# A Trainium2 kernel of four fused blocks: the engines' loops written out as straight code

## The reference

```python
# 1. attention, 16 heads of 8, LayerNorm on each head's q and k, causal
dot = jnp.einsum('bqhs,bkhs->bhqk', q, k) * scale
attn = jax.nn.softmax(jnp.where(causal, dot, -jnp.inf), axis=-1)
out = jnp.einsum('bhqk,bkhs->bqhs', attn, v).reshape(b, t, e) @ Wo + bo
# 2. soft mixture of experts, 8 experts x 64 slots
logits = jnp.einsum('bnd,esd->bnes', xn, sn)
dispatch = jax.nn.softmax(logits, axis=1)
combine = jax.nn.softmax(logits.reshape(b, n, e * s), axis=-1)
slots = jnp.einsum('bnd,bnes->besd', xn, dispatch)
h = gelu(jnp.einsum('besd,edh->besh', slots, w1) + b1)
out = jnp.einsum('bmd,bnm->bnd', (h @ w2 + b2), combine)
# 3. differential attention: softmax(q1 k1) - lam * softmax(q2 k2), times v, RMS norm
# 4. attention over the batch axis, then a routed mixture (top 2 of 8 experts, capacity 1280):
probs = softmax(x @ router_weight); top_p, top_i = top_k(probs, 2)
exp_out = gelu(exp_in @ moe_w1) @ moe_w2          # per expert
```

## Time and profile before

| | us |
|---|---|
| median of 3 runs (range) | 1091.5 (1090.92 to 1092.26) |
| profiled execution: span from first to last instruction | 1086.1 |
| PE busy | 919.8 |
| DVE busy | 712.3 |
| ACT busy | 625.7 |
| POOL busy | 569.8 |

### The profile page before, as it was taken

The page is one execution under the profiler, slowest core; times in us unless marked ns, Lnnn a source line. Parts: engine busy times, 40 slices in busy tenths (PEclk is TensorE's granted clock), DMA queues, the critical chain, the costliest instruction groups (busy, mean ns, idle before and its releaser), DMA issues.

```text
span 1086.1 us, 20632 instructions
## 1 busy us (share of the span) xinstructions
PE 919.8 (85%) x6577; PEld 615.8 (57%) x6614; DVE 712.3 (66%) x1512; ACT 625.7 (58%) x1129; POOL 569.8 (52%) x645
## 2 busy tenths in 40 slices
PE   7688879988999899899999868677788886999980
PEld 4366654477555555555555446454555655998870
DVE  6788852125777677677766565999857673646374
ACT  6466664421887687678778746344478664333320
POOL 3400019261675566656642217999306771888772
PEclk9899989999999999999999969879989998999995
DMA  5011111434010010100101049900011102223277
GB/s 144 1 78 78 77 79 58 135 128 135 21 31 21 22 30 21 31 21 21 30 21 30 2 79 149 298 11 0 1 39 43 51 28 79 83 78 92 73 204 219
DMA packets 83841, 74.46 MB, mean 69 GB/s; under 512 B 6786, under 2 KB 76876, under 8 KB 81712
## 3 DMA queue, kind: packets, MB, share of 16 engines
q1 hardware_dynamic: 73392, 64.03, 22.3%
q0 software_dynamic: 4608, 6.64, 1.9%
q10 hardware_dynamic: 5760, 2.70, 0.9%
HBM read 34.14 MB, written 33.70 MB: 62 GB/s over the span
## 4 chain that ended last, share of the span: by engine, by line
PE 32%; DVE 18%; POOL 10%; issue 9%; ACT 2%; DMA 1%; ACTq 0%; DVEq 0%; POOLq 0%
PE banks L2030 6%; PE banks L2002 5%; PE banks L2016 5%; POOL y_dram L975 4%; PE banks L2056 3%; DVE B_mneg L1150 2%; PE banks L2004 2%; DVE D_dmx L1282 2%; PE banks L2114 2%; PE banks L2069 2%; PE banks L2165 1%; DVE banks L1331 1%; DVE D_sc L1308 1%; POOL x L951 1%; DVE D_pr L1293 1%
## 5 line engine op out<-in xcount | busy, mean ns | idle before, releaser
L1150 DVE TENSOR_REDUCE B_mneg<-banks 128x2 f32<-128x256 f32 (+3 forms) x256 | 208.5, 824 | 76.9 <-PE banks L2004 68.3
L1669 ACT ACTIVATE B_pt<-banks 128x1024 f32<-128x1024 f32 (+3 forms) x256 | 178.7, 708 | 72.9 <-PE banks L2016 67.8
L792 POOL TENSOR_SCALAR_AFFINE_SELECT B_pt<-B_pt 128x512 f32<-128x512 f32 x128 | 81.2, 634 | 170.4 <-ACT B_pt L1669 161.3
L2002 PE MATMUL banks<-B_kp,B_qt 128*128 128x128 bf16 (+3 forms) x507 | 124.7, 299 | 1.8 <-DVE B_mneg L1150 0.6
L2016 PE MATMUL banks<-B_qt,B_kp 128*128 128x256 bf16 (+3 forms) x480 | 105.2, 297 | 12.1 <-issue 5.2
L2004 PE MATMUL banks<-B_mask_q,B_identb 128*128 128x128 bf16 x512 | 101.8, 219 | 0.7 <-issue 0.6
L2030 PE MATMUL banks<-B_pt,B_vp 128*32 128x512 f32 (+3 forms) x1024 | 95.5, 445 | 1.4 <-ACT B_ot L1675 0.7
L1819 ACT ACTIVATE F_gh<-banks 128x512 f32<-128x512 f32 (+1 forms) x96 | 50.0, 526 | 78.8 <-PE banks L2234 74.2
L930 POOL DMA_INDIRECT rows_dram<-F_xs,F_rowi x64 | 62.4, 975 | 60.2 <-issue 59.6
L2165 PE MATMUL banks<-D_qk 128*128 128x512 f32 x128 | 74.9, 671 | 10.2 <-DVE D_pr L1293 10.2
L975 POOL DMA_INDIRECT y_dram<-F_yo,F_ide x60 | 60.8, 1014 | 37.8 <-DVE F_yo L1510 17.4
(11 more groups left out here) (292 smaller groups left out, 2192.3 us busy)
## 6 DMA issues: line engine op xcount, KB each, us to landing
comb_dram<-C_comb SPq DMA_DIRECT2D x8, 1024.0 KB, 3.9
C_cst<-comb_dram SPq DMA_DIRECT2D x8, 1024.0 KB, 4.8
B_kp<-B_kt SPq DMA_DIRECT2D x64, 128.0 KB, 2.4
rows_dram<-D_zeros SPq DMA_DIRECT2D x8, 650.0 KB, 17.8
F_xe<-rows_dram SPq DMA_DIRECT2D x8, 650.0 KB, 3.9
C_w<-w_in SPq DMA_DIRECT2D x16, 256.0 KB, 2.9
y_dram<-D_zeros SPq DMA_DIRECT2D x2, 2048.0 KB, 19.0
F_gw<-mw_in SPq DMA_DIRECT2D x16, 256.0 KB, 3.0
```

The lines of the kernel that those rows point to most:

```text
L792: g.affine_select(out=w, in_=w, compare_op=ALU.is_ge, fill=0.0, base=0, pattern=[[0, G], [1, P]], channel_multiplier=-1).then_inc(B_md, 1)
L1150: v.tensor_reduce(mneg[:, g % 2, qt, 2 * hp:2 * hp + 2], banks2[pair_of_banks(item)][:, :, 0:(qt + 1) * P], X, ALU.max, negate=True).then_ ...
L1669: a.activation(pt[:, 2 * hp:2 * hp + 2, PT_AT[kt]:PT_AT[kt] + w], banks2[pair_of_banks(item)][:, :, 0:w], ACT.Exp).then_inc(B_ex, 1)
L2002: t_.matmul(dst, qt1[:, g % 2, hp, qt * P:(qt + 1) * P], kp[:, g % NG, hp, h, 0:(qt + 1) * P], start=True, stop=False)
```

## The change

All seventeen `Fori` loops, on SP, POOL, DVE, ACT and PE, become Python `for` loops, so that the bodies are written out once per iteration. The same items run in the same order with the same buffers, semaphores and counts; thresholds and addresses are constants. `Chain` loses its loop bookkeeping. `Rounds.place` now tells the last round by its number, where before any integer counted as that. The core of the diff (the other loops are edited the same way):

```diff
@@ class Chain
     def __init__(self, eng, sem):
-        self.eng, self.sem, self.start, self.n, self.it, self.per = eng, sem, 0, 0, 0, 0
-
-    def loop(self, it, per):
-
-        self.start, self.n, self.it, self.per = self.start + self.n, 0, it, per
-
-    def end_loop(self, times):
-        assert self.n == self.per, (self.n, self.per)
-        self.start, self.n, self.it, self.per = self.start + times * self.per, 0, 0, 0
+        self.eng, self.sem, self.n = eng, sem, 0
 
     def link(self, ins):
 
         self.n += 1
         ins.then_inc(self.sem, 1)
-        self.eng.wait_ge(self.sem, self.it * self.per + (self.start + self.n))
+        self.eng.wait_ge(self.sem, self.n)
...
+LAST_ROUND = B // 2 - 1
...
     def place(self, stream, it, item):
 
         names = self.streams[stream]
-        if isinstance(it, int) and it >= 0:
+        if it == LAST_ROUND:
             names = [x for x in names if x not in self.early]
         return names.index(item) + 1
...
             dve_round_c(-1, True)
-            with dve.Fori(0, B // 2 - 1) as it:
-                own.loop(it, 2 * (1 + 1 + 2))
+            for it in range(B // 2 - 1):
                 dve_round_c(it, False)
-            own.end_loop(B // 2 - 1)
             dve_round_c(B // 2 - 1, False, True)
...
-            with act.Fori(0, EXP // 2) as pr:
+            for pr in range(EXP // 2):
                 for par in range(2):
...
             pe_round(-1, True)
-            with pe.Fori(0, B // 2 - 1) as it:
+            for it in range(B // 2 - 1):
                 pe_round(it, False)
             pe_round(B // 2 - 1, False, True)
...
             pe_round_g(-1, True)
-            with pe.Fori(0, EXP // 2 - 1) as it:
+            for it in range(EXP // 2 - 1):
                 pe_round_g(it, False)
             pe_round_g(EXP // 2 - 1, False, True)
```

More of the change, by code:

```diff
@@ L625, in store_comb @@
                                  comb[:, par, :, :].rearrange("p m n -> p (m n)")).then_inc(C_cw[par], 16)
-            with sp.Fori(0, B // 2 - 1) as hb:
+            for hb in range(B // 2 - 1):
                 store_comb(hb)
             store_comb(B // 2 - 1)
-            with sp.Fori(1, EXP // 2) as pr:
+            for pr in range(1, EXP // 2):
                 for par in range(2):
@@ L661, in _ @@
             spread_keys(-1, True)
-            with sp.Fori(0, B // 2 - 1) as it:
+            for it in range(B // 2 - 1):
                 spread_keys(it, False)
@@ L859, in _ @@
             pool_round(-1, True)
-            with pool.Fori(0, B // 2 - 1) as it:
-                own.loop(it, 2 * 2 * 6)
+            for it in range(B // 2 - 1):
                 pool_round(it, False)
-            own.end_loop(B // 2 - 1)
             pool_round(B // 2 - 1, False, True)
@@ L1125, in _ @@
             dve.sem_inc(C_pp, 2)
-            with dve.Fori(0, EXP // 2) as pr:
+            for pr in range(EXP // 2):
                 for par in range(2):
@@ L1231, in _ @@
             dve_round(-1, True)
-            with dve.Fori(0, B // 2 - 1) as it:
-                own.loop(it, PG * 3 + 2 * 4)
+            for it in range(B // 2 - 1):
                 dve_round(it, False)
-            own.end_loop(B // 2 - 1)
             dve_round(B // 2 - 1, False, True)
@@ L1519, in _ @@
             dve_round_g(-1, True)
-            with dve.Fori(0, EXP // 2 - 1) as it:
-                own.loop(it, 2 * (2 * 3 + 2))
+            for it in range(EXP // 2 - 1):
                 dve_round_g(it, False)
-            own.end_loop(EXP // 2 - 1)
             dve_round_g(EXP // 2 - 1, False, True)
@@ L1623, in _ @@
             act_round_c(-1, True)
-            with act.Fori(0, B // 2 - 1) as it:
+            for it in range(B // 2 - 1):
                 act_round_c(it, False)
@@ L1820, in _ @@
             act_round_g(-1, True)
-            with act.Fori(0, EXP // 2) as it:
+            for it in range(EXP // 2):
                 act_round_g(it, False)
@@ L1933, in _ @@
             pe.sem_inc(C_ps, 2)
-            with pe.Fori(0, EXP // 2) as pr:
+            for pr in range(EXP // 2):
                 for par in range(2):
```

## The result

| | before | after |
|---|---|---|
| median, first comparison (4 runs each) | 1091.21 us (1088.66 to 1092.26) | 1074.25 us (1072.77 to 1076.21) |
| ratio after/before | | 0.985, interval 0.9833 to 0.9867 |
| profiled execution, span | 1086.1 us | 1073.3 us |
| profiled execution, whole time | | 1075.17 us |

The account below looks back on a forecast made before the run. It took router and attention as rings of TensorE, VectorE and ScalarE waiting on each other, and GpSimd as pacing routed experts. 6.4 + 2.0 + 0.3 + 0.2 = 8.9 us off 1091.5 gave 1082.6 us, range 1078.5 to 1088.5.

Parts of the forecast that it names:

- Attention: Attention stage: jumps, register work and batch seams together save 6.4 us, bounds 1.6 and 7.9.
- the seams: Attention, between batches: 1.64 us from TensorE's two jumps, plus 0.9 us from loop code at three seams.
- the three loop rounds outside the seams: Attention: register work ahead of waits and addresses goes, six half rounds at 0.65 us, 3.9 us.
- The first half of a round: Attention, DVE maximum to merged batch's turn: 43.39 us looped, 42.51 straight; 0.65 us saved, bounds 0 and 0.88.
- the second: Attention, other half round, 43.8 us, no straight counterpart: same kinds of waits, so also 0.65 us, bounds 0 and 0.9.
- something else is late there anyway: Attention, TensorE's two jumps: DVE's residual and statistics are late next, so 1.64 us is saved, not 5.0.
- Router: Router: address and loop-turn instructions on DVE go, 0.65 us per iteration, 2.0 us in all, bounds 0 and 3.8.
- Slot experts: Slot experts: table loads are covered; only register work before `C_pair` counts, 0.3 us, bounds 0 and 0.9.
- Routed experts: Routed experts: GpSimd sets the pace; only the way to its first scatter counts, 0.2 us, bounds 0 and 0.6.
- Rival 2: Attention and other loops: longer code needs new fetches, 7 exposed misses of 2.5 us, 17.5 us lost, 1100.1 us; chance 0.07.
- that remainder is outside the first and last instruction and I leave it as it is: Whole kernel: the 5.4 us between profiled span 1086.1 and median 1091.5 lies outside the span and stays.
- TensorE's granted clock: Whole kernel: given no term in the sum; no time was claimed for it.

Follow-up runs that it names:

- e3: TensorE's loops alone made straight code (router, slot experts, attention, routed experts), other engines' loops kept, against the kernel before: 1084.64 us beside 1089.77, ratio 0.9946.
- e1: Only the attention loops made straight code, on all five engines, against the kernel before: 1080.32 us beside 1089.77, ratio 0.9905.
- e5: Only the attention loops of VectorE, ScalarE, GpSimd and SyncE made straight, TensorE's kept, against the kernel before: 1084.77 us beside 1091.31, ratio 0.9953.
- e6: Only the router's loops made straight code, against the kernel before: 1091.73 us beside 1091.31, ratio 1.0006.
- e7: Apparently, by the order of the experiments: the changed kernel plus seven extra TensorE matmuls in two waits; 1074.51 us, ratio 0.9863 to the kernel before.
- b0: The kernel before, unedited, profiled and timed again: 1090.42 us over 12 executions, ratio 1.0008.
- e17: All loops straight except TensorE's attention loop, against the kernel before on the same chip: 1078.48 us beside 1090.88, ratio 0.9901.
- e2: Router, slot experts and routed experts made straight code, attention loops kept, against the kernel before: 1084.85 us beside 1089.77, ratio 0.9965.
- e13: The changed kernel, unedited, again on a slow chip, against the kernel before there: 1147.85 us beside 1169.12, ratio 0.9795.
- e9: The changed kernel, unedited, again on another slow chip, against the kernel before there: 1125.52 us beside 1161.09, ratio 0.9678.

## Why the prediction was right and wrong

**Attention, forecast 6.4, measured 6.4** in both pairs of traces (371.1 to 364.7, and 371.1 to 364.6 in the repeats). Its parts: the seams gained 1.10, 0.88 and 0.17, together 2.15, against 1.64 + 0.9 = 2.5; the three loop rounds outside the seams about 4.0, forecast 3.9, and the last round 0.3, for which the forecast had nothing. The first half of a round went from 43.39 us to 42.84, the second from 43.81 to 42.99: 0.55 and 0.82 us, where 0.65 was taken for each. So the sum is not luck, though its halves erred either way. The step "something else is late there anyway" was right and worth the most: 3.4 us of jump was worth 0.65 and 0.46 us alone (e3) and some 1.3 and 1.0 with the others straight (e1 against e5, its half clock taken off). Unforeseen was that TensorE's registers count for next to nothing and VectorE's for 2.25 of the 3.9 that e5 gives the four.

**Router, forecast 2.0, measured 1.9** and 2.04 in e6; rounds of 25.73 against "near 25.8". **Slot experts, 0.3, measured 0.5**; a pair takes 15.67 us, forecast 15.7, and of the eight table loads two are left. **Routed experts, 0.2:** not resolved. From the first turn of `F_xe` to the end it is 180.3 us before (905.8 to 1086.1) and 179.0 after; but e7 has 178.3, e1 180.2 and a second trace of before 178.9.

**Rival 2, code fetched anew, didn't happen** as a loss, though its premise held: in the attention rounds the second instruction queue brought 11 packets instead of 7, the four that were worked out, and no idle time put down to issue is over 0.6 us there (278 to 541 us of the changed kernel, queues, then the longest of the waits):

```profile
q14 instruction: 11, 0.09, 0.1%
```

```profile
PEld banks L2003 <- issue: 14.4, 23, 0.6
```

No fetch of the written-out code held an engine there for longer than that.

**What failed is the last step of the sum, and a term that it put at nothing.** The step: "that remainder is outside the first and last instruction and I leave it as it is." Outside are only 1.7 to 1.9 us (b0), in the first four executions of the changed kernel 1.7 to 2.1. The term: TensorE's granted clock, to which the sum gave no time at all, inside the profiled span or in its remainder. The 17.0 us between the medians divide so:

- 8.8 us are the terms of the sum, read in the traces.
- 4.0 us more the span fell by (12.8 in all). They lie outside attention: 2.6 ahead of it, where before has half clock at 160 and 226 us and the changed kernel from 53 to 60, and 1.4 behind 603 us. The second pair of traces (1085.6 and 1071.7) has 6.7 us ahead of attention, 2.4 of them from the terms, so 4.3 beyond them. These spells come and go between executions of one kernel, as below.
- 4.2 us are the remainder, which was to stay: the median of before lies 5.1 us over its profiled span, that of the changed kernel 0.95. As only 1.7 to 2.1 lie outside the span in either kernel, the profiled execution of before was shorter than its median and that of the changed kernel longer.

A part of the excess over the terms is half clock behind TensorE's two jumps: 2.2 us, an estimate (4.25 in e17 less 2.0 for the seams; in e17 all other engines are straight, and neither trace of the kernel before has this half clock). The medians bear it out that something beyond the terms goes with this loop. By the intervals, the kernels without it gained more than their terms: e1 7.7 to 12.9 us against 6.6 in the trace, e3 3.8 to 8.0 against 1.1. For those that keep it the terms are enough: e2 1.5 to 6.1 against 2.5, e5 2.5 to 7.9 against 3.9, e6 between 3.6 lost and 2.3 gained against 2.0.

What lies ahead of attention is shown in traces but not tied to a loop. Both traces of before have half clock at 160 and 225 us; e5, whose code up to there is that of before, has neither, and the changed kernel's repeat e13 has the one at 159. How often each comes in either kernel stays open, and with it what is left of the median gain, 5 to 6 us.

The forecast had TensorE's idle time in front of it, at clock 1.0 in the one execution profiled. It priced the idle time and not what may follow it. A rival "the clock falls behind the jump in other executions, and the change takes that away" with 1.5 to 2.5 us for each was missing. It would have carried the forecast to between 1077 and 1080, and the range's lower end to about 1073.5, which holds the measured 1074.25.

## What to carry to other kernels

A stall on TensorE has two prices: its own time, which was mostly hidden here because another engine is late at the same place, and the half clock that may follow it; one trace shows the second price only if it happens there. So before taking "time less profiled span" as fixed, compare the profiled execution's own time with its median. Written-out code paid here on the engine that others wait for (VectorE's address and threshold arithmetic) and on the one loop whose body is so long that the jump costs 3.4 us; a loop over a few instructions jumps in 0.21 us and may stay.

## What was not expected of the hardware

On two of the five chips of the experiments every kernel took 50 to 80 us longer, nearly all of it after about 820 us, where GpSimd scatters rows. Up to the end of attention the changed kernel's trace on one of them (e9) runs 1 to 3 us ahead of its first trace, on the other (e13) 3 us behind it. From 820 to 880 us the first trace, then the one with 1150.2 us of span (e13):

```profile
820.00:880.00 60.00, 50.47 (x248) 33.23 (x248) 42.70 (x150) 38.68 (x102) 45.82 (x47) 0.91 0.13 43
```

```profile
820.00:880.00 60.00, 34.37 (x147) 22.80 (x145) 27.91 (x104) 24.95 (x65) 28.25 (x30) 0.74 0.10 33
```

All engines do a third less there, and TensorE's clock falls with the idle time. It is not a slower pace but standstills of three engines at once: from 856 to 864 us of that trace TensorE and ScalarE have no instruction and VectorE one, while GpSimd goes on scattering; afterwards GpSimd idles (11.7 and 11.8 us, twice in these 60 us). The kernel before ran on those chips and lost more, so that the change was worth 35.6 and 21.3 us on them. What stalls there wasn't found, nor why the kernel before loses more.
